# Recurrent denominators on VectorE, and GpSimd's numerators held until the routing's second part is done

## The reference, cut to what matters

```python
exp_k = jnp.exp(k)
exp_k_v = exp_k * v
# conv_*: running sums over the rows, decayed by exp(-exp(w)) a row
denominator_out = (denominator - exp_k) / exp_w + exp_k * exp_u
numerator_out = (numerator - exp_k_v) / exp_w + exp_k_v * exp_u
return jax.nn.sigmoid(r) * numerator_out / denominator_out @ W_out.T
...
# _gate: scores per expert, two of four groups, then four experts
group_scores = jax.lax.top_k(sv, 2)[0].sum(-1)
top_groups = jax.lax.top_k(group_scores, TOPK_G)[1]
...
_, idx = jax.lax.top_k(masked, TOPK)
```

## Time and profile before

| | |
|---|---|
| time, median of 3 (lowest, highest) | 1114.01 us (1110.69, 1118.83) |
| the profiled execution's own time | 1122.04 us |
| its span, first to last instruction | 1120.2 us |
| PE busy (share of the span) | 995.2 us (89%) |
| DVE busy | 790.6 us (71%) |
| ACT (ScalarE) busy | 687.7 us (61%) |
| POOL busy | 633.4 us (57%) |
| mean granted TensorE clock | 0.960 |
| chain that ended last, by engine | PE 43%, DVE 38%, issue 9%, ACT 4%, POOL 2% |

### The profile page before, as it was taken

How to read it: one execution, slowest core, us unless ns; L and a number is a source line. 1 busy time by engine, 2 the same in 40 slices (tenths; PEclk the granted TensorE clock), 3 DMA queues, 4 the chain that set the end, 5 groups by cost and what they waited for, 6 DMA issues and landing times.

```text
span 1120.2 us, 21626 instructions
## 1 busy us (share of the span) xinstructions
PE 995.2 (89%) x6502; PEld 764.6 (68%) x6502; DVE 790.6 (71%) x1634; ACT 687.7 (61%) x2182; POOL 633.4 (57%) x683
## 2 busy tenths in 40 slices
PE   4689988998989899898898988989799999999996
PEld 2456666766667677676666766656688888887774
DVE  2377888889788898898879889875342222455687
ACT  1167765867658577675766766776355655666533
POOL 4664455756657567564666756313545555565653
PEclk8789999999889999999989999999999999999997
DMA  9614233443343431112211111112334554688764
GB/s 260 216 31 143 75 111 112 136 153 106 111 137 123 139 109 47 50 52 80 82 46 50 47 38 40 41 60 80 124 109 145 154 152 136 204 267 259 232 218 158
DMA packets 97871, 135.38 MB, mean 121 GB/s; under 512 B 11202, under 2 KB 83553, under 8 KB 97760
## 3 DMA queue, kind: packets, MB, share of 16 engines
q1 hardware_dynamic: 84704, 101.53, 29.5%
q0 software_dynamic: 13056, 32.47, 7.9%
HBM read 61.91 MB, written 76.23 MB: 123 GB/s over the span
## 4 chain that ended last, share of the span: by engine, by line
PE 43%; DVE 38%; issue 9%; ACT 4%; POOL 2%; DMA 1%; another core or an unknown queue 1%; SPq 1%; DVEq 0%; POOLq 0%; ACTq 0%
DVE Sc L1329 9%; PE four L848 6%; PE bT L848 6%; DVE nmx L1331 6%; PE four L889 6%; PE four L774 4%; PE bM L739 4%; PE bT L593 4%; DVE wkv L1306 3%; DVE st L1244 2%; PE bM L586 2%; PE bO L810 2%; ACT Sc L1069 2%; PE bU L579 2%; PE bU L680 2%
## 5 line engine op out<-in xcount | busy, mean ns | idle before, releaser
L1077 ACT ACTIVATE PT<-bT 128x512 f32<-128x512 f32 x256 | 151.8, 593 | 183.3 <-PE bT L593 181.6
L1069 ACT ACTIVATE Sc<-Sc,nmx 128x256 f32<-128x256 f32 x512 | 253.5, 500 | 8.2 <-DVE nmx L1331 8.2
L1732 POOL DMA_INDIRECT Yt<-PT,dests x150 | 149.4, 996 | 111.0 <-issue 72.9
L593 PE MATMUL bT<-idn,Sc 128*128 128x128 f32 x1024 | 162.5, 282 | 6.4 <-ACT PT L1077 5.3
L593 PEld LDWEIGHTS bT<-idn,Sc 128*128 128x128 f32 x1024 | 115.1, 142 | 73.1 <-issue 62.8
L1329 DVE TENSOR_SCALAR Sc<-four 128x1024 f32<-128x1024 f32 x128 | 155.1, 1212 | 11.9 <-PE four L774 4.7
L1331 DVE TENSOR_REDUCE nmx<-Sc 128x4 f32<-128x1024 f32 x128 | 156.2, 1220 | 4.4
L1715 POOL DMA_INDIRECT Xs<-x,slots x120 | 121.9, 1016 | 35.2 <-issue 18.6
L1069 ACT ACTIVATION_READ_ACCUMULATOR Sc<-Sc,nmx 128x1 f32 x512 | 98.7, 193 | 0.0
L1643 POOL TENSOR_TENSOR rstd<-vpe,mhalf 128x2 f32<-128x2 f32 x48 | 35.7, 743 | 100.4 <-DVE vpe L1252 100.3
L774 PE MATMUL four<-KT,QT 32*128 32x256 f32 x1024 | 78.9, 420 | 9.3 <-DVE Sc L1329 7.2
(11 more groups left out here) (230 smaller groups left out, 2134.4 us busy)
## 6 DMA issues: line engine op xcount, KB each, us to landing
Xs<-yg SPq DMA_DIRECT2D x16, 1768.0 KB, 7.7
xb<-Xs SPq DMA_DIRECT2D x152, 136.0 KB
yg<-Yt SPq DMA_DIRECT2D x27, 512.0 KB
W<-w SPq DMA_DIRECT2D x4, 1152.0 KB, 11.4
xTs<-xT SPq DMA_DIRECT2D x16, 256.0 KB, 2.9
x<-x SPq DMA_DIRECT2D x16, 256.0 KB, 2.9
Base<-stg SPq DMA_DIRECT2D x15, 256.0 KB
out<-acc SPq DMA_DIRECT2D x15, 256.0 KB
```

The source lines that it names most:

```text
L593: last = pe.transpose(dst[:, j, t * P:(t + 1) * P], src[:, t, j * P:(j + 1) * P], idn[:, :])
L1069: last = fn(Sc[:, n % 3, m, t, :], Sc[:, n % 3, m, t, :], ACT.Exp, bias=nmx[:, n % 3, m, t:t + 1], accum_out=rs[:, s % 2, t, h:h + 1])
L1077: fn(flat(PT[:, h % RING]), bT[:, :], ACT.Copy).then_inc(a_pt.sem, 1)
L1732: pool.indirect_dma_start(Yt, bass.IndirectOffsetOnAxis(ap=dests[:, i % IDS, b:b + 1], axis=0), y_rows(i)[:, b, :], None, bounds_check=SPA ...
```

## The change

The two GpSimd instructions of `sum_den` go. In their place VectorE makes the denominators itself, by two `scalar_tensor_tensor` instructions (one for each half of the channels, 128x256, exp u as a column of scalars), between `router(t, 0)` and the reciprocals. The event `g_den`, which counted both kinds of sums, is split into `d_den` (VectorE) and `g_num` (GpSimd). `sum_num` on GpSimd gets one more wait: in steps with a row T it starts only when `router(t, 1)` is through (`d_route`, 16 signals). The place of `sum_num` in GpSimd's order stays.

```diff
+            def sum_den(s):
+                dve.wait_ge(a_ek.sem, a_ek.at(s))
+                if s:
+                    dve.wait_ge(g_state.sem, g_state.at(s - 1))
+                for j in range(ND):
+                    last = stt(den[:, j, :], ek[:, j, :], eu[:, j:j + 1], Sd[:, j, :], ALU.mult, ALU.add)
+                last.then_inc(d_den.sem, 1)
+
             def invert(s):
-                dve.wait_ge(g_den.sem, g_den.at(s, 2))
+                dve.wait_ge(d_den.sem, d_den.at(s))
                 for j in range(ND):
                     dve.reciprocal(den[:, j, :], den[:, j, :]).then_inc(d_rden.sem, 1)
...
                 if B and g == 5:
+                    sum_den(b)
                     invert(b)
...
-            def sum_den(s):
-
-                pool.wait_ge(a_ek.sem, a_ek.at(s))
-                if s:
-                    pool.wait_ge(d_wkv.sem, d_wkv.at(s - 1))
-                by = eu[:, :].rearrange("p (j a) -> p j a", a=1).to_broadcast([P, ND, TOK])
-                pool.tensor_tensor(den, ek, by, ALU.mult).then_inc(g_den.sem, 1)
-                pool.wait_ge(g_den.sem, g_den.at(s, 1))
-                pool.tensor_tensor(den, den, Sd, ALU.add).then_inc(g_den.sem, 1)
...
                 pairs(4)
-                if B:
-                    sum_den(b)
                 send(s - 2, 2)
                 pairs(5)
                 send(s - 2, 3)
                 pairs(6)
                 if B:
+                    if T:
+                        pool.wait_ge(d_route.sem, d_route.at(t, ROUTER_SIGNALS[2]))
                     sum_num(b)
```

More of the change, by code:

```diff
@@ L303, in decoder_layer @@
         a_thr = event("a_thr")
-        g_den = event("g_den", 4)
+        d_den = event("d_den")
+        g_num = event("g_num", 2)
         g_state = event("g_state", 4)
@@ L1309, in finish_wkv @@
                 dve.wait_ge(a_thr.sem, a_thr.at(s))
-                dve.wait_ge(g_den.sem, g_den.at(s))
+                dve.wait_ge(g_num.sem, g_num.at(s))
                 stt(flat(num), flat(thr), 1.0, flat(num), ALU.add, ALU.mult).then_inc(d_num.sem, 1)
@@ L1680, in sum_num @@
                 by = eu[:, :].rearrange("p (j a) -> p j a", a=1).to_broadcast([P, ND, TOK])
-                pool.tensor_tensor(num, ekv, by, ALU.mult).then_inc(g_den.sem, 1)
-                pool.wait_ge(g_den.sem, g_den.at(s, 3))
-                pool.tensor_tensor(num, num, Sn, ALU.add).then_inc(g_den.sem, 1)
+                pool.tensor_tensor(num, ekv, by, ALU.mult).then_inc(g_num.sem, 1)
+                pool.wait_ge(g_num.sem, g_num.at(s, 1))
+                pool.tensor_tensor(num, num, Sn, ALU.add).then_inc(g_num.sem, 1)
             def state(s):
-                pool.wait_ge(g_den.sem, g_den.at(s))
+                pool.wait_ge(d_den.sem, d_den.at(s))
+                pool.wait_ge(g_num.sem, g_num.at(s))
                 by = decay[:, :].rearrange("p (j a) -> p j a", a=1).to_broadcast([P, ND, TOK])
```

## The result

The changed kernel takes **1065.55 us** (median of 4 runs, 1064.41 to 1066.71), the kernel before beside it 1115.82 (4 runs, 1110.69 to 1118.83). The ratio is 0.9554, with a 95% interval of 0.9514 to 0.9594: faster by 4.5%. The forecast was 1073, between 1061 and 1089.

A forecast was written before the change was run, and what follows sets the result against it. VectorE's routing was taken to bound each step up to L739, TensorE after it. Terms 20.0 + 17.2 - 10.0 + 4.5 = 31.7 us less, plus 9 for the clock: 1114 - 31.7 - 9 = 1073 us, range 1061 to 1089.

The forecast's parts named there:

- The hold-ups' cause and their price: VectorE's routing: small instructions held up by GpSimd's SBUF-reading sums; 20.0 us freed in the first part, 17.2 in the second.
- The reading of L1402: Routing's second part: L1402 ends at 324.83 us, GpSimd's L1681 at 324.79, so L1402 is held up by that sum.
- The sums on VectorE: Two added sums: 0.77 us a pair, between 0.62 (half of L1311) and 0.88 (line through L1456 and L1311); 10.0 us.
- rival 3: The stalls move: the two new sums on VectorE are held up in their turn, 16.5 us back, 1089; chance 0.08.
- rival 4: Slower: the two sums run at the reciprocals' pace, 3.44 us a pair, giving 1125; chance 0.03.
- The cover for the numerators: After the routing's second part: some 3 us of clip and shared expert hide GpSimd's numerators, else `finish_wkv` would be late.
- The start: Three steps without T, where VectorE waits for denominators: 4.5 us less, between 0 and 4.7; 16.5 us wait shrinks to some 12.
- The clock: TensorE at L739: shorter waits, 0.6 or 0.7 us, win back 11 of 13.2 us lost to half clock, 9 in the median.
- The range: Whole kernel: 1061 to 1089 us; the forecast's own range 1062 to 1082, rivals 1 and 3 reaching to 1089.
- Rival 1: At L739: the stalls go but the clock stays down, something else than the wait setting it; 1082; chance 0.15.
- Rival 2: Before L739: TensorE becomes the bound, so half the gain is won, 1098; chance 0.05.
- Rivals 3, 4 and 5: Last of these: hold-ups have another cause and stay, nothing done to the path; 1119 at most, within 1%; chance 0.03.

The follow-up runs named there:

- The memsets: Kernel before, GpSimd's two denominator operations replaced by four memsets of the same tile that read nothing, denominators left out: 1111.36 us, ratio 0.9886.
- the two halves: Two runs: changed kernel without the hold of the numerators, 1107.47 us; kernel before with that hold alone, 1090.68 us.
- the half without this wait: Changed kernel with denominators on VectorE, but GpSimd's numerators not waiting for the routing: 1107.47 us, ratio 0.9846; called the denominators alone further on.
- The delays: Changed kernel with a scratch VectorE reciprocal before the shared expert's second half: 128x192 in 13 steps 1110.74 us, 128x64 in 13 steps 1100.49, 128x192 in six steps 1096.12.
- chip B: Second of three chips used; the changed kernel run again unchanged there took 1064.81 us, the kernel before 1115.92.
- chip C: Third of three chips used; the changed kernel run a third time unchanged there took 1077.43 us, the kernel before 1122.69.
- the numerators alone: Kernel before with GpSimd's numerators held until the routing's second part is done, denominators staying on GpSimd: 1090.68 us, ratio 0.9702.

## Why the prediction was right, and where its sizes were off

- **The hold-ups' cause and their price: right.** 20.0 + 17.2 was forecast, 20.2 + 16.9 measured. The memsets showed the cause for the first part, and the two halves showed that each part hangs on its own pair of GpSimd's sums. The reading of L1402 passed over that it started 0.50 us before L1681 did; that stays open.
- **The sums on VectorE: mis-sized.** 0.77 us a pair was taken from the middle of 0.62 and 0.88; it is 0.88, the upper bound. 11.4 us, not 10.0. The line through L1456 and L1311 was the better guide than half of L1311. They were not held up (rival 3) and did not go the reciprocals' pace (rival 4). On the path their worth is smaller than their length, 4.1 us of 11.4, because TensorE is close behind.
- **The cover for the numerators: right.** GpSimd waits for L1412 for 48.8 us in 11 of the 13 steps, and this is charged to nobody, since `finish_wkv` never waits there; in the half without this wait the numerators came beside the second part, and 13.1 of its 16.9 us stayed lost.
- **The start: right.** 4.5 forecast, 4.2 to 5.6 measured. The 16.5 us before the reciprocals became 9.1 + 0.6, where I had said some 12.
- **The clock: right mechanism, too small, and this is the term that failed.** Forecast 11 in the profiled execution and 9 in the median. It was 12.4 at L740, all but 0.8 of the 13.2 us seen there, and 3.2 at L775, a line that I had not compared with anything: a spell of half clock does not end where L739 ends, it runs on into the scores. The 16 products of the scores right behind it, in the step of rows 2 and in the same step now:

```profile
331.82 2.09 PE L774 MATMUL four<-KT,QT 32*128 32x256 f32 x16
```

```profile
308.03 1.15 PE L775 MATMUL four<-KT,QT 32*128 32x256 f32 x16
```

I lowered the 11 to 9 because nothing but half clock seemed to vary by the 8 us between the profiled execution and the median. That step failed: ScalarE's two idle times, 6.67 and 4.1 us, vary by more from chip to chip, and the trace before had them. Behind it stood the wait, forecast at 0.6 to 0.7 us and measured at 0.87 to 1.02 in 11 of 13 steps: longer than I said, at the edge of what I called harmless, and still at full clock each time. The delays show how near the edge this is: with 0.4 us more of waiting in each step, 10.2 of the 12.4 us at L740 were gone (40.1 against 29.9). The forecast was right here with less margin than it claimed.
- **What is left: sizes, and the chip.** By rows the steps and the start are 41.3 + 5.6 = 46.9, against 31.7 + 9 = 40.7 forecast for the median, so the sizes were 6.2 us too low: 6.6 on the clock and 1.1 on the start, less 1.4 for the sums and 0.1 for the hold-ups. The rest of the gap in the profiles, 10.2 us around ScalarE's idle times, the unchanged program shows too, from one chip to another. In the medians on record the gain is 50.3 us (1115.82 to 1065.55), on chip B 51.1 and on chip C 45.3: the forecast of 41 was low, and 1073 lay above 1065.55, inside its range.
- **The range: luck at its low end.** The terms named for it, 2 us of clock, 2 of the sums' price and 3 of scatter, make 7 and not 11, so 1066. The measured 1065.55 is just below that, inside only what the range had without a reason, 1061 to 1066.
- **The rivals.** Rival 1 (the stalls go and the clock stays down) did not come: where the waits fell to about 0.9 us, in the changed kernel and with the numerators alone, L740 is at full clock, and with the denominators alone waits and half clock stayed together. Rival 2 stands next in line. Rivals 3, 4 and 5 found nothing.

## What to carry to other kernels

Look for small VectorE instructions that end when a large one of GpSimd ends: their busy time is then a wait, and busy less count times the shortest run prices it well (37.2 forecast, 37.1 measured). Moving work off GpSimd pays in full only if what GpSimd does next, now earlier, does not land on the next small instructions; here the cheap half, one wait on GpSimd, gave 31.6 of 41 us. And where TensorE waits about a microsecond for VectorE in each step, a microsecond more ahead of that wait can cost double, as it did here (2.1 to 2.7 times), so compare all of TensorE's later lines for half clock, not only the first.

## What the runs showed of the hardware that I had not expected

- Memsets on GpSimd (128x512, 524 ns) did not hold up the two-input instructions of VectorE beside them (192 ns); operations that read SBUF held up even one-input forms, a 128x8 cast among them, for up to 1.37 us in place of 0.16.
- A wait of 1.28 to 1.32 us before L740 was followed by half clock in seven of eleven steps, none of up to 1.22 was, though 2.58 was followed by full clock in the trace before.
- A 128x256 sum and product with a column of scalars, all in SBUF, takes 479 ns, and a pair in a row 0.88 us.
- The same program takes 1064.81 us on one chip and 1077.43 on another, and nearly the whole difference, 12.3 of 13.4 us of span, lies behind the last row of the mixer, around two idle times of ScalarE of 7.3 and 4.1 us that only the second chip's trace has.
